# Two stacked cross-attention layers in float32: the products as plain float32 matmuls in place of sums of fp32r parts

## The reference

```python
q, k_t, v_t = hidden @ Wq, text @ Wk, text @ Wv        # per layer; heads are slices of 16 columns
probs = softmax(q_h k_h^T * scale); text_out = probs v_h
ip_k, ip_v = ip @ Wk_ip, ip @ Wv_ip
# layer 0: one semantic term for all heads, from a softmax over the whole width
text_probs = softmax(q k_text^T * scale); sem = ((text_probs @ text) ip^T) * scale
# layer 1: one semantic term per head
qsem = l2norm(probs @ text_ehs); sem = qsem l2norm(ip)^T
ip_probs = softmax(q_h ip_k_h^T * scale + 0.5 * sem) * spatial_mask[:, None]
out = (text_out + ip_probs ip_v_h) @ Wout + bout + hidden
```

## Time and profile before

| | |
|---|---|
| median of 3 runs | 1665.95 us (1664.27 to 1666.03) |
| profiled execution, span | 1665.6 us |
| PE busy | 1599.7 us (96%), 14248 matmul records |
| DVE, ACT, POOL busy | 1376.6, 992.3, 844.8 us |
| mean granted TensorE clock | 0.981 |

### The profile page before, as it was taken

How to read it: one execution, slowest core, us unless ns; L and a number is a source line. 1 busy time by engine, 2 the same in 40 slices (tenths; PEclk the granted TensorE clock), 3 DMA queues, 4 the chain that set the end, 5 groups by cost and what they waited for, 6 DMA issues and landing times.

```text
span 1665.6 us, 42402 instructions
## 1 busy us (share of the span) xinstructions
PE 1599.7 (96%) x14248; PEld 1424.2 (86%) x14248; DVE 1376.6 (83%) x3937; ACT 992.3 (60%) x2044; POOL 844.8 (51%) x789
## 2 busy tenths in 40 slices
PE   6999999999999999998989999999999999999986
PEld 5888888888888888788878998989998989998866
DVE  4688788888888888867879998999999998998874
ACT  3455565555556555655656666666666666666651
POOL 3224422222222323424767676777667776777662
PEclk9999999999999999999999999999999999999988
DMA  8334444444444444542323332333233323332201
GB/s 223 97 105 121 129 121 124 124 129 125 120 129 124 124 128 122 144 123 75 112 88 87 100 95 80 102 106 99 66 109 102 100 67 101 101 103 63 79 22 43
DMA packets 204225, 175.31 MB, mean 105 GB/s; under 512 B 45441, under 2 KB 203531, under 8 KB 204011
## 3 DMA queue, kind: packets, MB, share of 16 engines
q1 hardware_dynamic: 204010, 172.60, 35.8%
HBM read 112.13 MB, written 60.38 MB: 104 GB/s over the span
## 4 chain that ended last, share of the span: by engine, by line
PE 88%; DVE 6%; issue 3%; DMA 1%; SPq 1%; ACT 1%; POOL 0%; DVEq 0%; POOLq 0%; ACTq 0%
PE MISC L103 26%; PE GP L103 20%; PE NAT L265 10%; PE TR L278 8%; PE PV L324 5%; PE PV L309 4%; PE PV L306 3%; PE PV L327 2%; PE MISC L227 2%; PE MISC L367 1%; DVE ZP L895 1%; PE MISC L368 1%; PE MISC L466 1%; DVE TMP L779 1%; PE MISC L388 1%
## 5 line engine op out<-in xcount | busy, mean ns | idle before, releaser
L540 ACT ACTIVATE P<-TA 128x512 f32<-128x512 f32 x320 | 202.6, 633 | 279.4 <-DVE TA L888 278.0
L984 POOL TENSOR_TENSOR ZS<-ZP 128x256 f32<-128x256 f32 x267 | 255.4, 957 | 210.4 <-DVE ZP L895 209.0
L265 PE MATMUL NAT<-KS,QS 65*128 65x256 f32 x1280 | 300.1, 317 | 3.6 <-DMA KS<-qk_parts 2.1
L103 PE MATMUL GP<-PH,GH 128*128 128x256 f32 (+1 forms) x960 | 248.8, 288 | 20.9 <-DVE ZP L895 19.9
L278 PE MATMUL TR<-QS,KS 69*128 69x256 f32 (+1 forms) x1280 | 259.9, 285 | 4.6 <-DMA QS<-max_rows 2.5
L783 DVE TENSOR_REDUCE MX<-NAT 128x2 f32<-128x504 f32 x320 | 216.6, 677 | 51.3 <-PE NAT L265 46.9
L901 DVE SCALAR_TENSOR_TENSOR PM<-P,PH 128x512 f32<-128x512 f32 x320 | 255.3, 798 | 0.0
L215 POOL TENSOR_TENSOR PARTS<-QKF,PARTS 112x508 fp32r<-112x508 f32 (+3 forms) x93 | 119.3, 1283 | 265.1 <-ACT PARTS L568 263.2
L265 PEld LDWEIGHTS NAT<-KS,QS 65*128 65x128 f32 x1280 | 201.2, 192 | 56.9 <-issue 42.1
L103 PE MATMUL GP<-PH,GL 128*128 128x256 f32 (+1 forms) x960 | 243.0, 281 | 0.0
L543 ACT ACTIVATE P<-TR 128x512 f32<-128x512 f32 x320 | 192.7, 602 | 74.3 <-PE TR L278 71.3
(11 more groups left out here) (253 smaller groups left out, 3886.9 us busy)
## 6 DMA issues: line engine op xcount, KB each, us to landing
QS<-qk_parts SPq DMA_DIRECT2D x480, 64.0 KB
KS<-qk_parts SPq DMA_DIRECT2D x480, 64.0 KB
qk_parts<-PARTS SPq DMA_DIRECT2D x128, 224.0 KB, 2.8
CT<-in_ctx_t SPq DMA_DIRECT2D x32, 512.0 KB, 3.9
qk_parts<-PARTS SPq DMA_DIRECT2D x64, 192.0 KB, 2.4
XT<-in_x_t SPq DMA_DIRECT2D x48, 112.0 KB, 2.6
XT<-x_t SPq DMA_DIRECT2D x48, 112.0 KB, 2.4
XB<-in_x SPq DMA_DIRECT2D x16, 320.0 KB, 4.1
```

The costliest lines, as they stand in the source:

```text
L103: ins = e.matmul(out, lhs, rhs, start=(n == 0), stop=(n == len(pairs) - 1))
L265: ins = e.matmul(NAT[s % 2][:, i * T:(i + 1) * T], QS[0:KQ, h, i * 128:(i + 1) * 128], KS[0:KQ, h, :], start=True, stop=True)
L540: e.activation(P[:, s % NP, :], TA[:, s % 2, :], ACT.Exp, scale=SCALE).then_inc(q["exp"], 1)
L984: e.tensor_tensor(ZS[s % NZ][:, :], ZP[:, s % 2, 0:S], ZP[:, s % 2, S:2 * S], ALU.add).then_inc(q["zs"], 1)
```

## The change

Every `product3` becomes `product` with plain float32 operands, the parts and the work that made them go, G and P enter the Gram form as they are, and XT and CT get two buffers each with a semaphore each. Freed weight buffers allow the weights of layer 1 to be loaded beside those of layer 0. In `gr`, TensorE now waits for the scaled context columns (`ctn`), which `cts` waited for before; its bank is free after the copy to VB (`vc`), and ACT copies G before VB.

```diff
-def product3(e, out, lhs, rhs, cut_l, cut_r, chunks):
-    return product(e, out, [(cut_l(lhs[i], c), cut_r(rhs[j], c)) for c in range(chunks) for i, j in ((0, 0), (1, 0), (0, 1))])
-    XT, XTS = sb("XT", [128, 3, S]), pair("XTS", [128, 3, S])
-    CT, CTS = sb("CT", [128, KC, T]), pair("CTS", [128, KC, T])
+    XT, CT = sb("XT", [128, 2, 3, S]), sb("CT", [128, 2, KC, T])
 # TensorE, Gram form of a head
-                    e.wait_ge(q["gl"], 3 * (b + 1))
-                e.wait_ge(q["ph"], s + 1)
+                    e.wait_ge(q["gh"], 3 * (b + 1))
+                e.wait_ge(q["exp"], S1 + s + 1)
                 if s:
                     e.wait_ge(q["zp"], s)
-                p0, p1 = PH[:, k, 0:S], PH[0:N2, k, S:2 * S]
-                product(e, GP[:, 0:S], [(GH[:, p, 0, :], p0), (GL[:, p, 0, :], p0)])
-                product(e, GP[:, S:2 * S], [(GH[:, p, 1, :], p0), (GL[:, p, 1, :], p0), (GH[0:N2, p, 2, :], p1),
-                                            (GL[0:N2, p, 2, :], p1)]).then_inc(q["gp"], 1)
+                p0, p1 = P[:, k, 0:S], P[0:N2, k, S:2 * S]
+                product(e, GP[:, 0:S], [(GR[:, p, 0, :], p0)])
+                product(e, GP[:, S:2 * S], [(GR[:, p, 1, :], p0), (GR[0:N2, p, 2, :], p1)]).then_inc(q["gp"], 1)
 # TensorE, per batch (k of stage 1, om, q; v and gr alike)
-                    product3(e, k[0:mn, S:S + NT], WK, CTS, lambda w, c: w[:, c, m0:m0 + mn], lambda x, c: x[:, c, 0:NT], KC).then_inc(q["qk"], 1)
+                    product(e, k[0:mn, S:S + NT], [(WK[1][:, c, m0:m0 + mn], CT[:, b % 2, c, 0:NT]) for c in range(KC)]).then_inc(q["qk"], 1)
-                    product3(e, k[:, 0:C], HT, WO, lambda x, c: x[0:CK, c, i * 128:(i + 1) * 128],
-                             lambda w, c: w[0:CK, c, :], 3).then_inc(q["om"], 1)
+                    product(e, k[:, 0:C], [(HT[0:CK, c, i * 128:(i + 1) * 128], WO[b // B][0:CK, c, :]) for c in range(3)]).then_inc(q["om"], 1)
-                    product3(e, k[0:mn, 0:S], WQ, XTS, lambda w, c: w[0:CK, c, m0:m0 + mn], lambda x, c: x[0:CK, c, :], 3)
+                    product(e, k[0:mn, 0:S], [(WQ[b // B][0:CK, c, m0:m0 + mn], XT[0:CK, b % 2, c, :]) for c in range(3)])
 # ACT, per head of stage 1
                     e.activation(P[:, s % NP, :], TR[s % 2][:, :], ACT.Exp, scale=SCALE).then_inc(q["exp"], 1)
-                    if s - S1 >= NS:
-                        e.wait_ge(q["gp"], s - S1 - NS + 1)
-                    e.wait_ge(q["exp"], s + 1)
-                    e.copy(PH[:, s % NS, :], P[:, s % NP, :]).then_inc(q["ph"], 1)
 # DVE, per head of stage 1
-                e.wait_ge(q["pm"], s + 1)
                 e.wait_ge(q["gp"], s + 1)
-                e.tensor_tensor(ZP[:, s % 2, :], GP[:, :], PM[:, s % 2, :], ALU.mult).then_inc(q["zp"], 1)
+                e.tensor_tensor(ZP[:, s % 2, :], GP[:, :], P[:, s % NP, :], ALU.mult).then_inc(q["zp"], 1)
-                e.scalar_tensor_tensor(PM[:, s % 2, :], P[:, (S1 + s) % NP, :], 2.0, PH[:, s % NS, :].bitcast(F32), ALU.mult,
-                                       ALU.subtract).then_inc(q["pm"], 1)
 # SP, loads (x of stage 0; context of stage 1)
-                e.wait_ge(q["xt_lo"], 3 * b)
+                e.wait_ge(q["qk"], 3 * (b - 1))
                 load_x(b)
-                e.wait_ge(q["ct_lo"], B + b)
-                if b == 0:
-                    e.wait_ge(q["g0"], B)
+                if b < 2:
+                    e.wait_ge(q["vm"], 3 * (B + b - 1))
+                else:
+                    e.wait_ge(q["gr"], 2 * (b - 1))
                 load_ctx(B + b)
```

More of the change, by code:

```diff
@@ L122, in sb @@
             return stack.enter_context(nc.sbuf_tensor(name, shape, dt))
[L124 to L133, removed]
+        return sb
+    sb = tiles(ctx)
+    WQ, WK, WV, WO = ([sb(f"{n}{i}", [128, k, C]) for i in range(2)] for n, k in (("WQ", 3), ("WK", KC), ("WV", KC), ("WO", 3)))
     IDENT, MASK, HALF = sb("IDENT", [128, 128]), sb("MASK", [128, 2]), sb("HALF", [128, NIP])
-    XT, XTS = sb("XT", [128, 3, S]), pair("XTS", [128, 3, S])
-    CT, CTS = sb("CT", [128, KC, T]), pair("CTS", [128, KC, T])
+    XT, CT = sb("XT", [128, 2, 3, S]), sb("CT", [128, 2, KC, T])
     QKF, PARTS = sb("QKF", [128, 3, 2 * S]), sb("PARTS", [128, 3, 2, 2 * S], F32R)
@@ L146, in build @@
     with ExitStack() as first:
[L147 to L150, removed]
+        sb = tiles(first)
+        WVI = sb("WVI", [128, KC, C])
         VA, TA, ST = sb("VA", [NT0, 2, H, SLOT]), sb("TA", [128, 2, 2 * S]), sb("ST", [128, 2, 2 * S])
@@ L158, in build @@
     with ExitStack() as second:
-        sb, pair = tiles(second)
-        PH, KMASK, KBD = sb("PH", [128, NS, 2 * S], F32R), sb("KMASK", [128, 8, 4]), sb("KBD", [128, 3, 8, 4])
+        sb = tiles(second)
+        KMASK, KBD = sb("KMASK", [128, 8, 4]), sb("KBD", [128, 3, 8, 4])
         VMASK, E21 = sb("VMASK", [80, C]), sb("E21", [128, SLOT])
-        sb("in_wvi", [128, 32])
+        sb("in_wvi", [128, KC * C - 480])
         SC, RZ = sb("SC", [128, 3, 2, 80]), sb("RZ", [128, 2, H])
@@ L416, in _ @@
                 e.wait_ge(*free)
-                product(e, k[0:NT0, 0:NI0], [(CT[:, c, 0:NT0], CT[:, c, NT0:T]) for c in range(KC)]).then_inc(q["g0"], 1)
+                product(e, k[0:NT0, 0:NI0], [(CT[:, b % 2, c, 0:NT0], CT[:, b % 2, c, NT0:T]) for c in range(KC)]).then_inc(q["g0"], 1)
             b = of0(t, AT0["tpt"])
@@ L450, in _ @@
                 if b is not None:
[L451 removed]
+                    k, free = take(("gr", b, n), (q["vc"], 2 * b + n + 1), t)
                     e.wait_ge(*free)
                     if n == 0:
[L454 removed]
+                        e.wait_ge(q["ctn"], b + 1)
+                        product(e, k[:, 0:T], [(CT[:, b % 2, c, 0:128], CT[:, b % 2, c, :]) for c in range(KC)]).then_inc(q["gr"], 1)
                     else:
[L456 removed]
+                        product(e, k[0:N2, 0:128], [(CT[:, b % 2, c, 128:NT], CT[:, b % 2, c, 128:T]) for c in range(KC)]).then_inc(q["gr"], 1)
             b = of1(t, AT1["scm"])
@@ L487, in _ @@
     def _(e):
-        e.wait_ge(q["w_q"], 48)
-        e.wait_ge(q["clear"], 1)
-        e.copy(WQ[0][0:CK, :, :], WQR[1][0:CK, :, :]).then_inc(q["w_hi"], 1)
-        e.wait_ge(q["x_in"], 48)
-        for c in range(3):
-            e.copy(XTS[0][0:CK, c, :], XT[0:CK, c, :]).then_inc(q["xt_hi"], 1)
         for t in range(T0, T1):
```

267 lines of the change are left out of this document (73 added, 194 removed).

## The result

The changed kernel takes 1890.39 us (median of 4 runs, 1888.93 to 1891.64) against 1665.99 us (1664.27 to 1669.31) for the kernel before on the same chip: ratio 1.1341, interval 1.1321 to 1.1362.

The account below looks back on a forecast made before the run. The prediction took TensorE to bound the kernel, full in the middle of both stages. Its sum was 1665.6 + 270.8 (products) - 2 (start) - 8 (handover) = 1926.4 us of span, so 1927 us measured, range 1902 to 1953.

Parts of the forecast that it names:

- Price of a plain record: On TensorE, a plain matmul record costs two clocks a column: about 0.216 us for 256 columns, 0.269 for 320.
- Rival (c): On TensorE, plain matmuls overlap on wide tiles and a product's two records share their time: 1468 us, chance 0.02.
- (d): The plain products are built in fp32r after all, 2080 records at about 0.13 us: 1270 us, chance 0.01.
- Weight loads: On TensorE, plain operands lose the quick weight load by the skill's rule, but by the trace this costs nothing.
- Gross sum of +270.8: TensorE's changed products go from 667.3 to 938.1 us, 39 of the growth in stage 0 and 231 in stage 1.
- So nearly every nanosecond that the change adds to TensorE shows: TensorE is full in mid-stage (197.2 and 198.9 of 200 us), so its added +270.8 us show nearly whole.
- There the engine isn't the bound, so zero: Taking PM's 256 us off DVE, PH off ACT and the low parts off POOL gains nothing in mid-stage.
- Handover, 8 us back: Between the stages TensorE waits 9.5 us for ZP and 1.9 for HTL; 8 of the 11.4 come back.
- Tail zero, clock zero: Tail: HTL leaves, output products lengthen, zero (-3 to +5); clock: 63 us at 1.2 GHz, zero (-16 to +6).
- Start -2: At the start two casts on ACT (1.16 and 0.94 us) leave the chain after the key weights land: -2 us.
- Rival (b): The GP bank becomes a turn-taking of GP and ZP; a third of 160 us shows: 1980 us, chance 0.04.
- Rival (a): All waits at start and handover and half the clock's cost come back, 12 + 16 more: 1902 us, chance 0.08.

Follow-up runs that it names:

- experiment 1: The kernel before without PM on DVE, ZP being GP times PH: 1653.37 us, ratio 0.9928.
- experiment 4: The kernel after with PH on ACT and PM on DVE computed again without a use: 1890.03 us, ratio 1.1343.
- experiment 8: The kernel after with x in both stages and stage 1's context loaded as late as a single buffer would ask for: 1893.41 us, one run.
- experiment 6: The kernel before with the NAT matmuls issued three times for 40 heads about the handover: 1672.08 us, ratio 1.0025.
- b_gram_one: The kernel before with one fp32r part of G in place of two and no PM: 1567.26 us, ratio 0.9401.

## Why the prediction was wrong, point by point

- **Price of a plain record: right.** 0.216 for 256 columns and 0.269 for 320, as forecast; GP six in 1.30 us; two thirds of the records in the four groups of products. Rival (c) is dead: no overlap. So is (d).
- **Weight loads: right.** The Trainium skill, "TensorE: Matmul & The Clock Gate", section "Weight-path perf modes — Fast Weight Load (FWL) and DoubleRow", would have had plain operands load more slowly; the trace doesn't show it. The loads of G take 189 ns on the mean as plain float32, for 191 in fp32r.
- **Gross sum of +270.8: nearly right.** What the table leaves for the prices is 0.1 to 0.3 us a batch of stage 1, some 2 to 5 us in all.
- **"So nearly every nanosecond that the change adds to TensorE shows": this is the step that failed.** It rested on 98.6 and 99.5% busy. The chain had 12% that was not TensorE's, 200 us, and I put it all at the start, handover and tail without cutting the view to mid-stage. There 0.55 us a batch of stage 0 and 0.6 of stage 1 were waits on DVE, 9 + 10 us, and in these places (11 batches of stage 0, 12 of stage 1) each time a piece of DVE was held up by a piece of POOL beside it.
- **"There the engine isn't the bound, so zero": wrong in its reason, small in size.** DVE with 18 us to spare in 200 still held TensorE up, by single pieces and not by its load; taking PM out is worth 13.5 us (experiment 1). In the kernel after PM and PH are indeed worth zero (experiment 4), because the plain products cover them. POOL's low parts went into the same zero; CTSL is behind the larger of the two waits, and what it is worth by itself no run shows.
- **Handover, 8 us back: mis-sized.** It was 24 (8 and the 16.2 of the table), and with the second buffers in it, up to 8 (experiment 8).
- **Tail zero, clock zero: mis-sized.** The tail gave 8 us. Low-clock time fell by 33 us, worth up to 17; the prediction had the -16 in its bounds but took zero. Its sum by the Trainium skill's rule was 1904 of span; the span is 1887.6, further the same way. (1904 is 1665.6 + 270.8 - 32 and leaves out the 10 us of waits; with them it is 1894.)
- **Start -2:** it was +1.1. The two casts left the chain, but loads of x and of the key weights for the other products are waited for (5.8 and 3.7 us).
- **Rival (b): didn't come.** GP waits for ZP 7.1 us in all.
- **Rival (a)** had the sign, and 25 us where 39 came beyond the forecast. Handover and tail, where it looked, gave 24 of them, and the start took 3; the other 17 came from the middle of the stages, where it had nothing. Its 1902 is a slip as well: 12 + 16 more would be 1899.
- **The range** was too narrow below: it let the ends vary and held the middle fixed, as the busy share said. Above, its terms (8 + 5 + 6 + 17) come to 1963 and not to the 1953 taken, which changes nothing here.

What stays open: how much of the handover's 16 us beyond the forecast is clock and how much waits. The clock's records allow 12; experiment 6 shows that clock and waits move together, and no run parted them. Open too is how much of the steady middle's relief is due to POOL's low parts going; each run either keeps XTSL and CTSL or drops them together with the parts of the products.

## What to carry to other kernels

Before adding work to the engine that bounds, cut the chain of waits to a stretch of steady state and see if it leaves that engine. If it does, the first added work can be free and the first removed work can bring nothing, even where the loss is only 1% of the time: here 5% of the chain was off TensorE, +18.6 us cost 0 and -28 us gave 5. Look also at the longest and shortest time of each piece on that chain: one that takes 0.32 us and sometimes 1.47 is held up by something, here by POOL. Price handover and tail apart, and let the range follow both.

## What the runs showed that I had not expected

- A matmul record's shown duration hides waits: with a step of 0.12 us and 0.28 shown, a loss of 0.37 left 0.22 in the waits. The Trainium skill warns of it in "Perfetto Trace Analysis", section "Identifying the Most-Contended Engine": the busy share of matmuls is not a good measure of how close TensorE is to its peak. The share of weight loads, one of the two measures that it offers in its place, doesn't tell the kernels here apart, though: 87% in stage 0 of before and 80% in that of after, and the second is the one that TensorE bounds alone.
- Some pieces of DVE are held up until the piece of POOL beside them is done or nearly so: FU (0.32 us alone, up to 2.04 beside CTSL), the second FU (0.26 and 1.35), MN (0.16 and up to 2.5), PM (0.68 and up to 1.89). ZP, TA and MX, which read PSUM, vary by less than 0.07 us. It goes the other way too: with PM put back in `a_dead_pm`, POOL's ZS takes 1.02 us on the mean for 0.73.
- 19 us of needless matmuls at the handover cost 4 us and took the low-clock time there from 27.3 to 17.
- Shorter products brought the low clock into mid-stage: `b_gram_one` has 3.4 us of it in every third batch of stage 1 from 991 us to 1432, and with them batches of 50.1 us between ones of 47.7 and 48.6.
